# Attention row maxima on one Trainium2 core: each piece waits for its own PSUM bank instead of a pair of pieces waiting for both

## The reference

```python
def _gqa(x, wq, wk, wv, wo):            # B=4, S=2048, 16 heads of 16, 4 key/value heads
    q = (x @ wq.T).reshape(B, S, 16, 16)
    k = repeat((x @ wk.T).reshape(B, S, 4, 16), 4, axis=2)
    v = repeat((x @ wv.T).reshape(B, S, 4, 16), 4, axis=2)
    attn = einsum('bqhd,bkhd->bhqk', q, k) * 0.25
    attn = where(tril, attn, -inf)
    attn = softmax(attn, axis=-1)        # needs the maximum of every row of scores
    return einsum('bhqk,bkhd->bqhd', attn, v).reshape(B, S, 256) @ wo.T
```

## Time and profile before

| what | value |
|---|---|
| median of 3 runs | 8745.64 us (8745.47 to 8752.05) |
| the profiled execution | 8750.53 us |
| its span, first to last instruction | 8748.8 us |
| TensorE busy in the span | 84% |
| VectorE busy in the span | 86% |
| ScalarE busy in the span | 58% |
| mean granted TensorE clock | 0.95 of 2.4 GHz |
| VectorE, line 833, whole span | 4840 reduces, 2915.6 us busy, 389.7 us idle before them |

### The profile page before, as it was taken

How to read it: one execution, slowest core, us unless ns; L and a number is a source line. 1 busy time by engine, 2 the same in 40 slices (tenths; PEclk the granted TensorE clock), 3 DMA queues, 4 the chain that set the end, 5 groups by cost and what they waited for, 6 DMA issues and landing times. The chain is left out here.

```text
span 8748.8 us, 137191 instructions
## 1 busy us (share of the span) xinstructions
PE 7384.9 (84%) x39098; PEld 2876.4 (33%) x39098; DVE 7557.3 (86%) x11017; ACT 5055.9 (58%) x7663; POOL 3676.0 (42%) x1812
## 2 busy tenths in 40 slices
PE   6788888889997888888878888888777888888799
PEld 3222222225543333333323333333542222222255
DVE  6898888878867999999979999999358988888888
ACT  3577777762235666666655555555224777777622
POOL 0010011100006999999969999999300100110000
PEclk8799999999999999999999999999987999999999
DMA  6001001012262222222223333333561011011122
GB/s 171 17 19 20 19 19 26 19 42 77 72 210 88 83 83 82 82 83 84 83 92 100 102 103 100 100 102 100 171 189 17 19 20 19 19 21 23 42 67 67
DMA packets 554170, 623.35 MB, mean 71 GB/s; under 512 B 205376, under 2 KB 363328, under 8 KB 549408
## 3 DMA queue, kind: packets, MB, share of 16 engines
q1 hardware_dynamic: 548896, 581.63, 22.8%
q0 software_dynamic: 4608, 33.56, 1.9%
HBM read 416.65 MB, written 163.76 MB: 66 GB/s over the span
## 5 line engine op out<-in xcount | busy, mean ns | idle before, releaser
L833 DVE TENSOR_REDUCE ffn_att_mx<-psum 128x1 f32<-128x512 f32 (+2 forms) x4840 | 2915.6, 655 | 389.7 <-PE psum L666 197.4
L794 ACT ACTIVATE ffn_att_e<-psum,unscale 128x1024 f32<-128x1024 f32 (+3 forms) x2560 | 2384.0, 983 | 843.9 <-PE psum L739 842.9
L632 POOL TENSOR_SCALAR_AFFINE_SELECT ffn_att_e<-ffn_att_e 128x512 f32<-128x512 f32 x512 | 324.6, 634 | 3125.8 <-ACT ffn_att_e L794 3125.8
L666 PE MATMUL psum<-ffn_att_k,ffn_att_q 48*128 48x512 f16 (+3 forms) x5384 | 989.1, 368 | 611.2 <-DVE ffn_att_mx L833 545.2
L1628 POOL TENSOR_TENSOR scan_r_h<-scan_r_h,scan_r_cs 128x1024 f32<-128x1024 f32 x512 | 1207.1, 2447 | 148.0 <-ACT scan_r_state L1791 144.7
L705 PE MATMUL psum<-ffn_att_e,ffn_att_v 128*32 128x512 f32 (+3 forms) x10240 | 1248.5, 558 | 10.0 <-issue 3.8
L1628 POOL TENSOR_TENSOR scan_f_h<-scan_f_h,scan_f_cs 128x1024 f32<-128x1024 f32 x512 | 1204.4, 2444 | 118.8 <-ACT scan_f_state L1791 116.1
L1707 PE MATMUL psum<-scan_f_h,ident 128*128 128x512 f32 x2048 | 989.0, 623 | 84.0 <-POOL scan_f_h L1628 83.1
L1707 PE MATMUL psum<-scan_r_h,ident 128*128 128x512 f32 x2048 | 975.0, 617 | 78.1 <-POOL scan_r_h L1628 77.5
L1831 ACT ACTIVATE psum<-scan_r_dt,scan_r_an 128x512 f32<-128x512 f32 x1024 | 698.1, 682 | 456.2 <-DVE scan_r_h L1923 456.0
L1831 ACT ACTIVATE psum<-scan_f_dt,scan_f_an 128x512 f32<-128x512 f32 x1024 | 697.6, 681 | 423.8 <-DVE scan_f_h L1923 423.3
(11 more groups left out here) (240 smaller groups left out, 9216.5 us busy)
## 6 DMA issues: line engine op xcount, KB each, us to landing
scan_f_cs<-scan_f_bcd SPq DMA_DIRECT2D x264, 256.0 KB, 3.2
scan_r_cs<-scan_r_bcd SPq DMA_DIRECT2D x264, 256.0 KB, 3.3
scan_f_bs<-scan_f_bcd SPq DMA_DIRECT2D x82, 256.0 KB, 3.5
scan_r_bs<-scan_r_bcd SPq DMA_DIRECT2D x82, 256.0 KB, 3.5
scan_f_win<-xp SPq DMA_DIRECT2D x18, 1036.0 KB, 6.6
scan_r_win<-xp SPq DMA_DIRECT2D x18, 1036.0 KB, 7.0
ffn_att_q<-q_parts SPq DMA_DIRECT2D x144, 128.0 KB, 2.9
mamba_out_ys<-yz SPq DMA_DIRECT2D x18, 1024.0 KB, 7.3
```

Of the source, the lines that this page charges most:

```text
L632: nc.gpsimd.affine_select(out=part, in_=part, compare_op=ALU.is_ge, fill=0.0, base=0, pattern=[[0, REP], [1, P]], channel_multiplier=-1).t ...
L666: ins = nc.tensor.matmul(psum[:, turns[hh], j * w:(j + 1) * w], q[at, i // HALF, pair, i % HALF * P:(i % HALF + 1) * P], k[at, c * P:c * P ...
L794: nc.scalar.activation(E[:, s % PB, 2 * hp:2 * hp + 2, off:CH], psum[:, 2 * hp:2 * hp + 2, off:CH], ACT.Exp, scale=unscale[:, 0:1]).then_i ...
L833: nc.vector.reduce_max(mx[:, hh * 2 + pairs[0]:hh * 2 + pairs[1], i // HALF, i % HALF, c // TT], psum[:, turn, 0:(pairs[1] - pairs[0]) * w ...
```

## The change

`maximum` now makes one piece instead of two: it takes one bank and the half of the array that the piece's `hh` names, issues that piece's score matmuls and its own two mask matmuls, and signals `m_ps` once. `maxima` walks over pieces singly, so that each waits for its own bank. The prologue loop does the same. The banks, the planner's split of pieces to steps, the number and shapes of matmuls, and all other engines' programs are as before. The file is nine lines shorter, so that 666 becomes 665, 674 becomes 669, and later lines move by nine (739 is 730, 705 is 696, 833 is 824, 794 is 785).

```diff
-                def maximum(par, n, turns):
+                def maximum(par, n, turn):
 
                     q, k = Q[par], K[par]
-                    i, c, w, pairs, _ = pieces[n]
+                    i, c, w, pairs, hh = pieces[n]
+                    at, rows_at = slice(hh * ROWS, hh * ROWS + PARTS), slice(hh * ROWS, (hh + 1) * ROWS)
+                    is_diag = c + TT > i
                     for j, pair in enumerate(range(*pairs)):
-                        is_diag = c + TT > i
-                        for hh in range(2):
-                            at = slice(hh * ROWS, hh * ROWS + PARTS)
-                            ins = nc.tensor.matmul(psum[:, turns[hh], j * w:(j + 1) * w],
-                                                   q[at, i // HALF, pair, i % HALF * P:(i % HALF + 1) * P], k[at, c * P:c * P + w],
-                                                   start=True, stop=not is_diag, tile_position=(hh * ROWS, 0))
-                            if pair == pairs[1] - 1 and not is_diag:
-                                ins.then_inc(m_ps, 1)
+                        ins = nc.tensor.matmul(psum[:, turn, j * w:(j + 1) * w],
+                                               q[at, i // HALF, pair, i % HALF * P:(i % HALF + 1) * P], k[at, c * P:c * P + w],
+                                               start=True, stop=not is_diag, tile_position=(hh * ROWS, 0))
                         for z in range(2 * is_diag):
-                            for hh in range(2):
-                                at = slice(hh * ROWS, (hh + 1) * ROWS)
-                                ins = nc.tensor.matmul(psum[:, turns[hh], (j + 1) * w - P:(j + 1) * w], pick[at, 1 - hh + z, :],
-                                                       mask[at, 1 - hh + z, :], start=False, stop=z == 1,
-                                                       tile_position=(hh * ROWS, 0))
-                                if pair == pairs[1] - 1 and z == 1:
-                                    ins.then_inc(m_ps, 1)
+                            ins = nc.tensor.matmul(psum[:, turn, (j + 1) * w - P:(j + 1) * w], pick[rows_at, 1 - hh + z, :],
+                                                   mask[rows_at, 1 - hh + z, :], start=False, stop=z == 1, tile_position=(hh * ROWS, 0))
+                    ins.then_inc(m_ps, 1)
 
-                    for (kind, n), other in zip(todo[::2], todo[1::2]):
+                    for kind, n in todo:
...
                         bank_is_free(first, it, (kind, n))
-                        bank_is_free(first, it, other)
-                        maximum(par if kind == "tail" else (par + 1) % NBUF, n,
-                                (turn_bank(first, (kind, n)), turn_bank(first, other)))
+                        maximum(par if kind == "tail" else (par + 1) % NBUF, n, turn_bank(first, (kind, n)))
...
-                for n in range(0, T, 2):
-                    if n:
-                        pe.wait_ge(m_red, max(n - 1, 1))
-                    maximum(0, n, (5 + n % 3, 5 + (n + 1) % 3))
-                    if n == NP0:
+                for n in range(T):
+                    if n >= 3:
+                        pe.wait_ge(m_red, n - 2)
+                    maximum(0, n, 5 + n % 3)
+                    if n == NP0 + 1:
                         turn_maxima(0, 0, BANK_O)
```

## The result

The changed kernel takes 8677.58 us (median of 6 runs, 8669.37 to 8688.95) against 8747.53 us (6 runs, 8740.50 to 8755.05): ratio 0.9919, 95% interval 0.9907 to 0.9931. Its profiled execution took 8674.45 us (span 8672.7), 76 us less than the one before, with a mean granted clock of 0.955.

What follows compares the result with a forecast made beforehand. VectorE was taken to bound the prologue, with neither VectorE nor TensorE far ahead in the steps. Order +34.2, prologue gaps -15.6 and clock -5 gave +13.6 us on the median 8745.64: 8759 us, range 8712 to 8785.

Steps and rivals of the forecast that it cites:

- those 48 of 72 pairs I cost at nothing: Pairs off the diagonal: TensorE waits before them anyway, so a separate wait gains and costs 0 us.
- -15.6: Both prologues: VectorE's gaps at late first diagonal pieces close, 7.8 us of 9.9 each, 15.6 us saved.
- What the new order costs: Diagonal pairs in the steps: one half's matmuls after the other's add 1.07 us an iteration, +34.2 us over 32.
- place A: End of the second query block: longer diagonal pairs make a piece 0.51 us late for VectorE.
- B: End of the fourth query block: the 256-wide pair delays scores, `weighted` and a reduce, costing 0.41 us.
- C: At 1651.29 us: TensorE's 0.25 us wait hides only part of the first chain; 0.15 us reach `weighted`.
- the walk's covers: Diagonal pairs of one iteration: most of the 24 are covered by a wait before or 0.35 us and more behind.
- fourth rival: Mask weight loads: none hidden behind its own half's matmul, about 5.5 us an iteration, +160: 8906 us; chance 0.03.
- In the same walk the earlier first pieces give nothing in the steps: Steps: a gap closed by an earlier first piece returns at the next pair, which hangs on `weighted`; gain 0.
- Rival 1: Steps: half of VectorE's 105.6 us of gaps ended by mask matmuls close too, -34: 8711 us; chance 0.18.
- The clock, -5: Off the diagonal in the steps: TensorE active longer between waits may keep its clock up; bounds 0 and 25, taken -5 us.
- theory C: Theory set up for the experiments, not in the prediction: the granted clock carries most of the 70 us gain.

Runs made afterwards that it cites:

- Fillers over 48 rows: Kernel before, with two more matmuls (512 and 384 wide, 48 rows, into an unread bank) behind each prologue pair: 8736.78 us, ratio 0.9993.
- fillers over 128 rows: Kernel before, with two matmuls (384 wide, all 128 rows, into an unread bank) behind each prologue pair: 8717.46 us, ratio 0.9962.

## Why the prediction was wrong

**The bound of the prologue: right. Its gain: half.** VectorE was the bound, the clock stayed at 0.50, and the gaps at mask matmuls closed. "All such gaps of a prologue sum to 7.0 + 2.9 = 9.9 us", of which 7.8 would close, is what the kernel with single pieces on the diagonal alone gained (8.5). The other 8 us come from "those 48 of 72 pairs I cost at nothing", carried over to the prologue. The step that failed is "Off the diagonal it does not: TensorE waits before such pairs and the 32 reduces run on without a gap". That holds where a pair is fast enough, as at 2.4 GHz, and the earlier trace rows show only that. At 1.2 GHz, off the diagonal, the first reduce of a pair started 0.784 us behind the reduce before it, and the second 0.608 behind the first; single, both are 0.598. Little of this is an idle time that a list of waits has: gaps too short to be listed sum to 3.1 us a prologue, and 4.0 us are rows that overlapped less, since a reduce's row is 0.68 us long and the next one can start 0.598 behind its start. The earlier trace rows had it in sight: 4.07 us for 6 reduces, 0.68 each, beside the 0.61 of the earlier trace rows. I took both for VectorE's own pace ("0.6 to 0.7 us"). The term was -15.6 and measured -32.

**"What the new order costs", +34.2: the largest error.** The step that failed is "Now two such chains stand in a row, and only the last mask matmul of the first (0.06 us) runs beside the second". The two halves run beside each other across the two masks in between, so the 384 and 512 wide pairs cost nothing and place A (0.51) does not exist. Where six matmuls make a piece, the order does cost, 0.5 to 0.6 us an iteration with pair waits. B and C are such pairs, forecast at 0.41 and 0.15. With single waits this cost lies beneath the gain. Whether the walk's covers were right stays open.

The rule that I named as the fourth rival (the Trainium skill, TensorE: Matmul & The Clock Gate, Part 3, what overlaps and what doesn't) did not come out either. The same passage says that matmuls keep program order in their starts. The rows of 1613.41 above speak against it for matmuls of different halves: the second half's score starts ahead of the first half's masks.

**"In the same walk the earlier first pieces give nothing in the steps": wrong.** The steps gave 42 us by the timed ratio. By the traces it is 34 us for single pieces (25 on the diagonal) and 10 for the second stop behind the loop turn, which no term of the sum had. By the count above, over half of the 34 lie in the short stretches at 1.2 GHz, where the 0.78 us intervals of the prologue stand with pair waits, and 0.60 with single ones. Rival 1 (8711) was the nearest, with its sign right and its mechanism half right: the listed gaps at masks did not shrink (51.0 before, 53.9 now); what shrank are intervals ahead of first pieces, most of them too little to be seen in that list.

**The clock, -5: no change that the runs show.** Over the six runs of the changed kernel the mean granted clock is 0.949 to 0.955; over the runs of the kernel before that the experiments were compared with it is 0.945 to 0.952. So the rise from 0.950 to 0.955 between the two profiled executions is within what single executions differ by. The long gap of the earlier trace rows occurs in 23 of 30 iterations (each attention's last left out) where it was in 17, but in other traces with pair waits it occurs in 17 to 23 as well. With the prologue at 0.50 in both kernels, theory C falls: the clock sets what a pair wait costs, but nothing here shows that the change moved the clock.

**What would show it.** The prologue was 16 us shorter, not 8; at the place of the earlier trace rows the rows of 665 and 669 do not alternate singly; pair to scores stayed at 0.28 and 0.34; before the third reduce there is still no gap (12 reduces run on from 1615.55), where 0.4 was forecast; the full steps kept their length (2.49 us). Two signs of being wrong did not show: two masks of one half are 0.06 us apart, as before, and the prologue's clock is 0.50. The third did: an iteration is shorter than before, 3261.3 / 32 = 101.9 to 3215.8 / 32 = 100.5 us in the mean. No sign named the prologue's own pace.

## What to carry to other kernels

Divide the length of a producer's or consumer's group of rows by its count in each stretch, and compare it with the same instruction's best pace elsewhere: a loss of 0.1 us a piece is in no list of waits, and can lie in rows that overlap less. A wait that covers two buffers costs nothing while the producer is fast enough to fill both in one consumer's step, and its price appears where the producer runs at its lower clock or starts late; single waits or more buffers cure it alike. Before costing an order of instructions in two halves of the array as a chain, look at whether rows of the two halves already overlap across other instructions, and when a difference of 10 us in a hardware loop has no cause in the code, look at the first microseconds behind its turn and at the instruction packets there.

## What the runs showed of the hardware

- Matmuls of the other half of the array start ahead of matmuls that precede them in the program. A second piece of three matmuls starts at once, ahead of two masks of the first (1613.41 us); one of six only behind the first piece's third matmul (1665.97 us, 0.19 us behind the pair's start), ahead of the other three.
- Fillers over 48 rows, with TensorE busy 84.79 of 88.5 us, left the granted clock at 0.50; fillers over 128 rows, with TensorE busy 54.44 of 75 us, had it at 0.96.
- Reduces of 128x512 from PSUM follow each other every 0.598 us, though the row of one is 0.68 us long.
- A second stop in TensorE's issue behind a loop turn (1.1 to 1.9 us in the kernel before, 10 us in all). It ends 1.20 to 1.53 us behind the landing of an instruction packet, and comes and goes with code elsewhere in the program.
